# Splitting the virtual node's inner row over two PSUM banks, with three identity products behind it, in a four-network graph kernel

## The chip, the cores and the metric

The kernel is written in Bass and runs on one core of one Trainium2 chip. The metric is the device time of one launch in microseconds (us); lower is better.

## The reference, cut to what matters

Four graph networks run one after the other on 256 nodes of 512 features and 8192 edges, each between a layer norm and a residual add. Only the first one is touched by the change. It has seven layers; in each layer but the first, a "virtual node" gathers all nodes and gives one row of 512 numbers back to every node, ahead of the edge aggregation:

```python
for l in range(1, L):                       # L = 7
    h2 = relu(_ln(h, norm_g[l-1], norm_b[l-1]))
    vn_tmp = segment_sum(h2, batch) + vn                        # one row: sum over the nodes
    vn_hid = relu(_ln(vn_tmp @ vn_W1[l-1] + vn_b1[l-1], vn_g[l-1], vn_beta[l-1]))
    vn = vn_hid @ vn_W2[l-1] + vn_b2[l-1]
    h2 = h2 + vn[batch]
    h = _genconv(h2, src, dst, gcn_W[l], gcn_b[l]) + h          # softmax aggregation over edges, then a 512x512 product
```

All nodes are in segment 0 here, so `vn` is one row. Everything is float32.

## The kernel before, in words

Nodes lie in two tiles of 128 (`NT = 2`), features in four chunks of 128 (`CT = 4`). Adjacency is a dense 256x256 count matrix `cnt`, so that each sum over edges is a matrix product. Each engine has a program of its own, written out by hand in order, and they meet only through semaphores; SyncE (SP) issues the weight loads. There is no planner: what an engine does next is the next line of its program. In the listing all products of TensorE (PE) go through the helper `mm` and so carry line 762, all row picks of VectorE (DVE) line 1212.

One layer l (1 to 6) of the first network, `layer0` on each engine, goes like this:

1. PE begins the row `vn @ W1 + b1`: the bias (`vn_row_bias`) and chunk 0 of `vn` are already in the bank `row_bank(odd)` since the layer before; `vn_row_part(l, odd, 1, CT)` adds chunks 1 to 3. The column of `vn` is broadcast to a 128x128 stationary matrix, so every partition gets the whole row of 512.
2. `turn` transposes the normalised nodes `xn` (L797), tile by tile, as DVE has them ready (L1142). ScalarE (ACT) applies gain, bias and relu into `hT` and sums each chunk over the nodes into `hsum` (L645).
3. PE adds `hsum @ W1` to the row: four products of 512 columns, each with two records in the trace (tile `hsum`). Behind them it sets the bias of the next layer's row in the other bank (tile `ones`, one active row).
4. DVE, meanwhile, takes the maximum of `hT` over the nodes (L1226) and adds a bias (L1231). When the row is whole (`vn_hidden`) it takes its statistics (L1233, L1235), gives the variance to GpSimd (POOL) for the inverse root (L1236, L559), and picks from the row, which every partition has in full, each partition's own four numbers: `own_columns`, four multiply-and-sum instructions against the identity (L1212), each with a record that reads the accumulator. Three small operations follow (L1238, L1241, L1243), and `vhid` is ready (`vn_act`).
5. PE computes `vhid @ W2` in two halves of 256 columns, banks 2 and 3 (tile `vhid`, 16 records), each half raising `vn_half`.
6. For each half DVE picks `vn`, forms the shifts and the operand `md` (L1258); PE transposes `md` (`turn_md`, L871), and exponentials, the sums over edges, and the layer's 512x512 product (`conv`, banks 4 and 5) follow. DVE adds the result to `h` (L1148), tile 0 first, takes its statistics (L1115), and the next layer begins.

PE's wait between steps 4 and 5 is a wait for the chain of DVE. `keep_busy(bank, n)` exists already, for other places: n products of the identity with 256 columns into a bank that nobody reads.

Of the kernel before, what the change touches and what calls it, by code (L numbers as in the profile page):

```python
# [9 lines left out]
ALU = mybir.AluOpType  # L10
ACT = mybir.ActivationFunctionType
AX = mybir.AxisListType

P = 128
N = 256
NT = N // P
D = 512
CT = D // P
E = 8192
ET = E // P  # L20
LAYERS = 7
# [38 lines left out]
HALFWAY = 5  # L60
INDEG = 5
FILL_FIRST = 6

LN_EPS = 1e-5
MSG_EPS = 1e-7
# [32 lines left out]

TR_L2 = LAYERS
VN_OUT = 2  # L100


class Steps:
# [5 lines left out]
    def link(self, ins):  # L109

        self.mark(ins)
        self.await_marked()
# [19 lines left out]
def gnn_stack_kernel(nc, A, out):  # L132
    COL, NCOL_A, NCOL_B = column_table()
    ctx = ExitStack()
    with ctx:
        def sb(name, shape, dt=F32):
            return ctx.enter_context(nc.sbuf_tensor(name, shape, dt))
# [100 lines left out]
        vn = sb("vn", [P, CT])  # L238
        vhid = sb("vhid", [P, CT])
        vcen = sb("vcen", [P, CT])  # L240
        vst = sb("vst", [P, 6])
        vmv = sb("vmv", [P, 2])
        vvar = sb("vvar", [P, 2])
        scrap = region(5)[:, 0:CT * P].rearrange("p (c n) -> p c n", c=CT)
# [99 lines left out]
        def row_bank(odd):  # L344

            return 6 + odd
# [21 lines left out]
        def _(sp):  # L368
# [65 lines left out]
            with sp.Fori(1, LAYERS - 1) as l:  # L434
                conv_weights(l)

                sp.wait_ge(vn_hidden, l)
                sp.dma_start(wbuf[1], rows(A["L0_gnn_vn_W1"][bass.ds(l, 1)].rearrange("a k n -> (a k) n"))).then_inc(w_in[1], 16)
                sp.wait_ge(vn_half, l * 2)
                sp.dma_start(wbuf[2], rows(A["L0_gnn_vn_W2"][bass.ds(l, 1)].rearrange("a k n -> (a k) n"))).then_inc(w_in[2], 16)  # L440
# [2 lines left out]
            load_tab(0, 0)  # L443
            load_tab(1, 0)

            sp.wait_ge(vn_hidden, LAYERS - 1)
            load_w(1, A["L1_gnn_m_w1"][0], None)
            sp.wait_ge(vn_half, (LAYERS - 1) * 2)
            load_w(2, A["L1_gnn_m_w2"][0], A["L1_gnn_m_b2"][0])
# [310 lines left out]
        def _(pe):  # L760
            def mm(o, lhsT, rhs, start, stop):
                return pe.matmul(o, lhsT, rhs, start=start, stop=stop)  # L762
# [29 lines left out]
            def turn(tr, ready, value):  # L792

                for t in range(NT):
                    pe.wait_ge(ready, value + (t + 1))
                    for c in range(CT):
                        ins = pe.transpose(chunks(0)[:, c, t * P:(t + 1) * P], xn[:, t, c * P:(c + 1) * P], ident[:])  # L797
                        if t == NT - 1 and c % 2:
                            ins.then_inc(tr_done, 1)
# [20 lines left out]
            def column(col, c):  # L820

                return col[:, c:c + 1].to_broadcast([P, P])

            def vn_row_bias(l, odd):
                pe.wait_ge(b1_in, 16)
                mm(PS[:, row_bank(odd), :], ones[0:1, :], b1_rows[:, bass.ds(l * D - D, D)], True, False)

            def vn_row_part(l, odd, lo, hi):
                pe.wait_ge(w_in[1], l * 16)
                pe.wait_ge(vn_set, l * 2 - 1 if hi <= 2 else l * 2)  # L830
                for c in range(lo, hi):
                    mm(PS[:, row_bank(odd), :], column(vn, c), wbuf[1][:, c, :], False, False)

            def keep_busy(bank, n):

# [3 lines left out]
            def layer0(l, odd, first, last):  # L839
                if not first:  # L840
                    vn_row_part(l, odd, 1, CT)
                turn(l, ln_out, l * 2)
                if first:
                    keep_busy(4, FILL_FIRST)
                    pe.wait_ge(cnt_set, NT)
                    for s in range(NT):
                        ins = mm(PS[:, INDEG, 0:N], ones[:], cnt[:, s, :], s == 0, s == NT - 1)
                    ins.then_inc(indeg_done, 1)
                if not first:
                    for c in range(CT):  # L850
                        pe.wait_ge(hT_ready, l * CT + (c + 1))
                        ins = mm(PS[:, row_bank(odd), :], column(hsum, c), wbuf[1][:, c, :], False, c == CT - 1)
                    ins.then_inc(vn_hidden, 1)
                if not last:
                    vn_row_bias(l + 1, 1 - odd)
                if not first:
                    pe.wait_ge(w_in[2], l * 16)
                    pe.wait_ge(vn_act, l)
                    for b in range(2):
                        for c in range(CT):  # L860
                            ins = mm(PS[:, VN_OUT + b, 0:N], column(vhid, c), wbuf[2][:, c, b * N:(b + 1) * N],
                                     c == 0, c == CT - 1)
                        ins.then_inc(vn_half, 1)

                def turn_md(b):
                    pe.wait_ge(md_ready, l * 2 + (b + 1))
                    if b:
                        pe.wait_ge(mex_ready, l * 2 + 1)
                    for c in range(2):
                        for t in range(NT):  # L870
                            ins = pe.transpose(halves(row_bank(odd))[:, t, c * P:(c + 1) * P],  # L871
                                               md[:, 2 * b + c, t * P:(t + 1) * P], ident[:])
                    ins.then_inc(mdT_done, 1)

                def gather(bank, val, ready, done, b):
                    pe.wait_ge(ready, l * 2 + (b + 1))
                    for c in (2 * b, 2 * b + 1):
                        for t in range(NT):
                            ins = mm(chunks(bank)[:, c, :], val[:, t, c * P:(c + 1) * P], cnt[:, t, :], t == 0, t == NT - 1)
                    ins.then_inc(done, 1)  # L880

                turn_md(0)
                if not last:
                    vn_row_part(l + 1, 1 - odd, 0, 1)
                gather(0, ex, ex_ready, den_done, 0)
                turn_md(1)
                gather(2, mex, mex_ready, num_done, 0)
                gather(0, ex, ex_ready, den_done, 1)
                gather(2, mex, mex_ready, num_done, 1)

                if first:
                    pe.wait_ge(cond_s, 1)
                    mm(PS[0:NC, row_bank(0), 0:N], fw2[:], cz, True, True).then_inc(cond_b, 1)
                pe.wait_ge(w_in[0], l * 32 + 32)
                for b in range(2):
                    pe.wait_ge(z_ready, l * 2 + (b + 1))
                    for t in range(NT):
                        for c in (2 * b, 2 * b + 1):
                            ins = mm(PS[:, 4 + t, :], z[:, c, t * P:(t + 1) * P], wbuf[0][:, c, :], c == 0, c == CT - 1)
                        if b:  # L900
                            ins.then_inc(conv_done, 1)
# [202 lines left out]
        def _(dve):  # L1104
# [103 lines left out]
            def own_columns(bank, into, first, n):  # L1208

                for k in range(n):  # L1210
                    c = first + k
                    ins = dve.tensor_tensor_reduce(out=scrap[:, c, :], in0=PS[:, bank, k * P:(k + 1) * P], in1=ident[:],  # L1212
                                                   scale=1.0, scalar=0.0, op0=ALU.mult, op1=ALU.add, accum_out=into[:, c:c + 1])
                return ins
# [4 lines left out]
            def layer0(l, odd, first):  # L1219
# [3 lines left out]
                def par(name, at=0, n=CT):  # L1223
                    return cols[:, bass.ds(l * CT + (COL[name] - CT + at), n)]

                link(dve.tensor_reduce(hmax[:], hT[:], AX.X, ALU.max))  # L1226
                if first:
                    dve.tensor_copy(vn[:], cols[:, COL["vn_emb"]:COL["vn_emb"] + CT]).then_inc(vn_set, 2)
                    dve.wait_ge(vn_set, 2)
                else:  # L1230
                    link(dve.tensor_tensor(hmax_b[:], hmax[:], par("vn_b2"), ALU.add))  # L1231
                    dve.wait_ge(vn_hidden, l)
                    link(dve.bn_stats(vst[:], PS[:, row_bank(odd), :]))  # L1233
                    carry()
                    link(dve.bn_aggr(vmv[:], vst[:]))  # L1235
                    dve.tensor_scalar(vvar[:, 0:1], vmv[:, 1:2], LN_EPS, None, ALU.add).then_inc(vn_var, 1)  # L1236
                    link(own_columns(row_bank(odd), vcen, 0, CT))
                    link(dve.scalar_tensor_tensor(out=vcen[:], in0=vcen[:], scalar=vmv[:, 0:1], in1=par("vn_g"),  # L1238
                                                  op0=ALU.subtract, op1=ALU.mult))
                    dve.wait_ge(vn_est, l)  # L1240
                    link(dve.scalar_tensor_tensor(out=vhid[:], in0=vcen[:], scalar=vvar[:, 1:2], in1=par("vn_beta"),  # L1241
                                                  op0=ALU.mult, op1=ALU.add))
                    dve.tensor_scalar(vhid[:], vhid[:], 0.0, None, ALU.max).then_inc(vn_act, 1)  # L1243

                for b in range(2):
                    two = slice(2 * b, 2 * b + 2)
# [364 lines left out]
```

## Time and profile before

| | |
|---|---|
| median of 3 runs | 847.8 us (846.3 to 848.04) |
| the profiled execution | 845.63 us, its span 843.5 us |
| mean granted TensorE clock in it | 0.98 |
| PE busy | 779.4 us (92% of the span) |
| DVE busy | 601.8 us (71%) |
| first network, layers 1 to 6 | about 57 to 260 us of the span |

Times in rows are us from the start of the span unless marked ns. PE's records are modelled at their ends (a record lasts until its result has drained, so neighbours overlap), and a busy PE may run at half rate: the granted clock says so, 1.00 for 2.4 GHz and 0.50 for 1.2 GHz.

### The profile page before, as it was taken

To read this page: it belongs to the slowest core of one execution; us is meant where nothing else is said; L and a number is where in the kernel's file an instruction comes from. 1 tells how busy PE (TensorE), PEld (TensorE's weight loads), DVE (VectorE), ACT (ScalarE), POOL (GpSimd) and SP (SyncE) were. 2 spreads that over 40 slices of the span, in tenths; PEclk is the share of its full clock that TensorE was granted. 3 is DMA by queue.
4 is the path that set the end of the run, shared out by engine and by line. 5 is a ranking of instruction groups with operands and counts; after the bars stand their busy time and mean duration, and the time that the engine had idled before them with its cause. 6 is when DMAs were issued, how large, how long until landed. Compare 5 with 4: busy or idle time off the path is not lost.

```text
span 843.5 us, 10707 instructions
## 1 busy us (share of the span) xinstructions
PE 779.4 (92%) x3028; PEld 507.7 (60%) x3028; DVE 601.8 (71%) x1569; ACT 219.9 (26%) x458; POOL 127.5 (15%) x150
## 2 busy tenths in 40 slices
PE   6898898898888999999999999789999999999968
PEld 2556365364465765666667564466686585685753
DVE  8876575765767534544453563699999999999995
ACT  7632123122220311311311311502503404305200
POOL 5000000000011000000000001631351261341000
PEclk9899899999999999999999999999999999999989
DMA  5912314224131333423333100661632443330000
GB/s 165 347 63 100 113 52 159 86 76 162 62 126 70 122 109 119 162 99 137 119 112 113 63 1 16 194 214 51 187 113 79 133 138 101 103 97 0 1 1 25
DMA packets 39335, 88.39 MB, mean 105 GB/s; under 512 B 3986, under 2 KB 4319, under 8 KB 39295
## 3 DMA queue, kind: packets, MB, share of 16 engines
q1 hardware_dynamic: 34656, 72.72, 25.4%
q0 software_dynamic: 4640, 15.21, 6.1%
q8 instruction: 18, 0.29, 0.1%
q14 instruction: 21, 0.17, 0.1%
HBM read 86.86 MB, written 1.05 MB: 104 GB/s over the span
## 4 chain that ended last, share of the span: by engine, by line
PE 70%; DVE 14%; issue 11%; DVEq 3%; POOL 1%; ACT 1%; ACTq 0%; POOLq 0%
PE PS L762 41%; PE PS L1071 15%; PE PS L1057 11%; DVE big L1521 2%; DVE h L1148 1%; DVE tail L1512 1%; PE PS L922 1%; PE PS L771 1%; DVE x L1584 1%; DVEq L1484 1%; DVEq L1488 1%; PE PS L967 1%; PE PS L871 1%; PE PS L797 1%; DVE xn L1361 1%
## 5 line engine op out<-in xcount | busy, mean ns | idle before, releaser
L762 PE MATMUL PS<-big 128*128 128x512 f32 (+1 forms) x368 | 137.5, 524 | 1.9 <-DVE big L1412 1.7
L1512 DVE SCALAR_TENSOR_TENSOR tail<-big,coef 128x448 f32 (+3 forms) x208 | 125.1, 614 | 4.8 <-issue 4.5
L1521 DVE TENSOR_TENSOR big<-big,tail 128x448 f32 (+3 forms) x208 | 115.3, 554 | 3.6 <-DVE tail L1512 2.5
L762 PEld LDWEIGHTS PS<-big 128*128 128x128 f32 x368 | 67.4, 190 | 64.1 <-issue 54.8
L762 PE MATMUL PS<-hT,big 128*128 128x256 f32 (+1 forms) x512 | 87.0, 329 | 4.4 <-ACT hT L685 4.4
L583 POOL DMA_INDIRECT big<-h_rows,src_i x58 | 75.7, 1304 | 83.4 <-PE PS L1057 60.8
L762 PEld LDWEIGHTS PS<-hT,big 128*128 128x128 f32 x512 | 77.5, 191 | 15.2 <-ACT hT L685 7.3
L553 POOL TENSOR_TENSOR rstd<-var,minus_half 128x1 f32<-128x1 f32 x34 | 20.5, 605 | 417.3 <-DVE var L1122 417.2
L1057 PE MATMUL PS<-big,hotd_more 128*128 128x512 f32 x152 | 66.0, 592 | 0.0
L1071 PE MATMUL PS<-hotd_more,tail 128*128 128x256 f32 x280 | 63.1, 379 | 0.0
L1071 PE MATMUL PS<-hotd_more,prods 128*128 128x256 f32 x260 | 58.6, 379 | 0.0
L1071 PEld LDWEIGHTS PS<-hotd_more,tail 128*128 128x128 f32 x280 | 53.4, 191 | 7.4
L741 ACT ACTIVATE big<-consts 128x3584 f32<-128x3584 f32 x5 | 16.0, 3191 | 158.0 <-DVE big L1521 147.7
L1071 PEld LDWEIGHTS PS<-hotd_more,prods 128*128 128x128 f32 x260 | 49.4, 190 | 6.7
L762 PE MATMUL PS<-cnt,big 128*128 128x256 f32 x224 | 51.4, 382 | 0.8 <-ACT big L654 0.8
L1057 PEld LDWEIGHTS PS<-big,hotd_more 128*128 128x128 f32 x152 | 28.9, 190 | 36.4 <-issue 36.4
L1148 DVE TENSOR_TENSOR h<-PS,h 128x512 f32<-128x512 f32 x26 | 17.9, 689 | 44.3 <-PE PS L762 44.1
L762 PEld LDWEIGHTS PS<-cnt,big 128*128 128x128 f32 x224 | 41.4, 190 | 10.5 <-ACT big L654 5.5
L762 PE MATMUL PS<-big,hT 128*128 128x512 f32 x96 | 43.3, 597 | 2.6 <-ACT hT L685 2.0
L1377 DVE TENSOR_SCALAR big<-PS,cols 128x256 f32<-128x256 f32 x16 | 7.0, 479 | 52.7 <-PE PS L762 52.7
L1071 PE MATMUL PS<-xn,tail 128*128 128x256 f32 x128 | 32.8, 401 | 12.6 <-DVE tail L1531 11.5
L762 PE MATMUL PS<-big,vhid 128*128 128x256 f32 x96 | 29.9, 481 | 13.9 <-DVE vhid L1243 13.9
(208 smaller groups left out, 1063.7 us busy)
## 6 DMA issues: line engine op xcount, KB each, us to landing
big<-in_edge_attr_dram SPq DMA_DIRECT2D x32, 512.0 KB, 3.7
big<-in_L_gnn_vn_W_dram SPq DMA_DIRECT2D x12, 1024.0 KB, 5.3
big<-in_L_gnn_m_w_dram SPq DMA_DIRECT2D x8, 1024.0 KB, 5.4
big<-in_L_gnn_gcn_W_dram SPq DMA_DIRECT2D x7, 1024.0 KB, 5.3
big<-in_L_gnn_wv_dram SPq DMA_DIRECT2D x4, 1024.0 KB, 5.3
big<-in_L_gnn_wq_dram SPq DMA_DIRECT2D x4, 1024.0 KB, 5.4
big<-in_L_gnn_wk_dram SPq DMA_DIRECT2D x4, 1024.0 KB, 5.5
big<-in_L_gnn_wo_dram SPq DMA_DIRECT2D x4, 1024.0 KB, 5.3
```

The source lines that it names most:

```text
L553: pool.tensor_tensor(rstd[:, t:t + 1], var[:, t:t + 1], minus_half[:, t:t + 1], ALU.pow).then_inc(ln_est, 1)
L583: pool.indirect_dma_start(out=part[SOURCE_AT[g]][:, j, :], out_offset=None, in_=h_rows, in_offset=bass.IndirectOffsetOnAxis(ap=src_i[:, ti ...
L741: act.activation(cut, zero.to_broadcast([P, ZERO_CUT * D]), ACT.Copy).then_inc(acc_zero, 1)
L762: return pe.matmul(o, lhsT, rhs, start=start, stop=stop)
L771: ins = pe.matmul(PS[:, 2 + s, 0:N], hot_s[:, k, s * P:(s + 1) * P], hot_d[:, k, :], start=False, stop=True, skip_group_check=True)
L797: ins = pe.transpose(chunks(0)[:, c, t * P:(t + 1) * P], xn[:, t, c * P:(c + 1) * P], ident[:])
L871: ins = pe.transpose(halves(row_bank(odd))[:, t, c * P:(c + 1) * P], md[:, 2 * b + c, t * P:(t + 1) * P], ident[:])
L1057: ins = pe.matmul(PS[:, t, :], hotd(j)[:, t * P:(t + 1) * P], part[SUM_AT[g]][:, j, :], start=g == 0 and j == 0, stop=True, skip_group_che ...
L1071: ins = pe.matmul(set_bank(SETS - SETS_OF[g] + i), prods[n % 2][:, j, :], hotd(j), start=g == 0 and j == 0 and SETS - SETS_OF[g] + i != 3, ...
L1148: link(dve.tensor_tensor(to[:, t, :], PS[:, bank + t, :], to[:, t, :], ALU.add))
L1512: dve.scalar_tensor_tensor(out=prod[:, slot, tiles, :], in0=xs[:, tiles, bass.ds(i1, EXT)], scalar=coef[:, row:row + 1], in1=xe[:, tiles, ...
L1521: dve.tensor_tensor(o, o, prod[:, slot, tiles, :], ALU.add)._wait_ge(path_step, max(product_at[slot], added_at[0])).then_inc(path_step, 1)
```

## The change

The row of step 3 is computed as two halves of 256 columns. The first stays in `row_bank(odd)`, the second goes to bank 4 (`VN_SECOND`), whose last reader in the layer before is DVE's residual add of tile 0. Bias and the `vn` part of the second half (five products of 256 columns) are computed ahead of `turn`, after a wait for the statistics of tile 0 (`st_set`). The `hsum` products come in the order first half, second half, first, second, first, first, second, second, and each half raises `vn_hidden` once. DVE takes statistics and own columns of the first half while the second is under way, then the statistics of the second, the aggregate of both, and the own columns of the second. The maximum over `hT` and the bias add move behind `vhid`. PE gets three identity products ahead of its wait for `vhid` (bank 2, which the products of `vhid` overwrite). SP's waits count to double the number.

```diff
+FILL_ROW = 3
+VN_SECOND = 4
-        vst = sb("vst", [P, 6])
+        vst = sb("vst", [P, 2, 6])
-                sp.wait_ge(vn_hidden, l)
+                sp.wait_ge(vn_hidden, l * 2)
-            sp.wait_ge(vn_hidden, LAYERS - 1)
+            sp.wait_ge(vn_hidden, 2 * (LAYERS - 1))
...
             def vn_row_bias(l, odd):
-                mm(PS[:, row_bank(odd), :], ones[0:1, :], b1_rows[:, bass.ds(l * D - D, D)], True, False)
+                mm(PS[:, row_bank(odd), 0:N], ones[0:1, :], b1_rows[:, bass.ds(l * D - D, N)], True, False)
...
                 for c in range(lo, hi):
-                    mm(PS[:, row_bank(odd), :], column(vn, c), wbuf[1][:, c, :], False, False)
+                    mm(PS[:, row_bank(odd), 0:N], column(vn, c), wbuf[1][:, c, 0:N], False, False)
+
+            def vn_second_half(l):
+
+                pe.wait_ge(st_set, l * 2 + 1)
+                mm(PS[:, VN_SECOND, 0:N], ones[0:1, :], b1_rows[:, bass.ds(l * D - D + N, N)], True, False)
+                for c in range(CT):
+                    mm(PS[:, VN_SECOND, 0:N], column(vn, c), wbuf[1][:, c, N:2 * N], False, False)
...
                 if not first:
                     vn_row_part(l, odd, 1, CT)
+                    vn_second_half(l)
                 turn(l, ln_out, l * 2)
...
-                    for c in range(CT):
-                        pe.wait_ge(hT_ready, l * CT + (c + 1))
-                        ins = mm(PS[:, row_bank(odd), :], column(hsum, c), wbuf[1][:, c, :], False, c == CT - 1)
-                    ins.then_inc(vn_hidden, 1)
+                    for c, half in ((0, 0), (0, 1), (1, 0), (1, 1), (2, 0), (3, 0), (2, 1), (3, 1)):
+                        if half == 0:
+                            pe.wait_ge(hT_ready, l * CT + (c + 1))
+                        ins = mm(PS[:, VN_SECOND if half else row_bank(odd), 0:N], column(hsum, c),
+                                 wbuf[1][:, c, half * N:(half + 1) * N], False, c == CT - 1)
+                        if c == CT - 1:
+                            ins.then_inc(vn_hidden, 1)
                 if not last:
                     vn_row_bias(l + 1, 1 - odd)
                 if not first:
+                    keep_busy(VN_OUT, FILL_ROW)
                     pe.wait_ge(w_in[2], l * 16)
                     pe.wait_ge(vn_act, l)
...
-                link(dve.tensor_reduce(hmax[:], hT[:], AX.X, ALU.max))
                 if first:
+                    link(dve.tensor_reduce(hmax[:], hT[:], AX.X, ALU.max))
...
                 else:
-                    link(dve.tensor_tensor(hmax_b[:], hmax[:], par("vn_b2"), ALU.add))
-                    dve.wait_ge(vn_hidden, l)
-                    link(dve.bn_stats(vst[:], PS[:, row_bank(odd), :]))
+                    dve.wait_ge(vn_hidden, l * 2 - 1)
+                    dve.bn_stats(vst[:, 0, :], PS[:, row_bank(odd), 0:N])
+                    own_columns(row_bank(odd), vcen, 0, 2)
+                    dve.wait_ge(vn_hidden, l * 2)
+                    link(dve.bn_stats(vst[:, 1, :], PS[:, VN_SECOND, 0:N]))
                     carry()
-                    link(dve.bn_aggr(vmv[:], vst[:]))
+                    link(dve.bn_aggr(vmv[:], vst[:, :, :].rearrange("p a b -> p (a b)")))
                     dve.tensor_scalar(vvar[:, 0:1], vmv[:, 1:2], LN_EPS, None, ALU.add).then_inc(vn_var, 1)
-                    link(own_columns(row_bank(odd), vcen, 0, CT))
+                    link(own_columns(VN_SECOND, vcen, 2, 2))
...
                     dve.tensor_scalar(vhid[:], vhid[:], 0.0, None, ALU.max).then_inc(vn_act, 1)
+                    link(dve.tensor_reduce(hmax[:], hT[:], AX.X, ALU.max))
+                    link(dve.tensor_tensor(hmax_b[:], hmax[:], par("vn_b2"), ALU.add))
```

## Rows read from the trace of the kernel before

**Rows 1.** The page: the span, and the granted clock in 40 slices.
```profile
span 843.5 us, 10707 instructions
...
PEclk9899899999999999999999999999999999999989
```

**Rows 2.** Waits, layers 1 to 6: in total, times, longest.
```profile
PE PS L762 <- DVE vhid L1243: 13.9, 6, 3.1
```

**Rows 3.** Timeline of layer 3, from the hsum products to the transposes of md.
```profile
129.82 3.70 PE L762 MATMUL PS<-big,hsum 128*128 128x512 f32 x8 [0.74 <-ACT hT L645]
...
131.43 1.22 DVE L1226 TENSOR_REDUCE hmax<-hT 128x4 f32<-128x1024 f32 x1 [3.07 <-ACT hT L645]
...
133.45 1.12 PE L762 MATMUL PS<-big,ones 1*128 x2
133.62 0.70 DVE L1233 BATCH_NORM_STATS2 vst<-PS 128x6 f32<-128x512 f32 x1 [0.66 <-PE PS L762]
...
134.81 0.55 POOL L559 TENSOR_TENSOR vvar<-vvar,minus_half 128x1 f32<-128x1 f32 x1 [7.24 <-DVE vvar L1236]
...
136.66 3.69 PE L762 MATMUL PS<-big,vhid 128*128 128x256 f32 x16 [2.09 <-DVE vhid L1243]
138.66 0.29 DVE L1212 CUSTOM_DVE_ANT_0 big<-PS,ident 128x128 f32<-128x128 f32 x1 [2.15 <-PE PS L762]
...
140.66 0.65 PE L871 MATMUL PS<-ident,big 128*128 128x128 f32 x4 [0.31 <-DVE big L1258]
```

**Rows 4.** Timeline, layers 1, 2, 6: products of vhid, transposes of md, DVE's third pick.
```profile
69.12 5.38 PE L762 MATMUL PS<-big,vhid 128*128 128x256 f32 x16 [2.22 <-DVE vhid L1243]
74.34 0.60 PE L871 MATMUL PS<-ident,big 128*128 128x128 f32 x4
...
74.54 0.29 DVE L1212 CUSTOM_DVE_ANT_0 big<-PS,ident 128x128 f32<-128x128 f32 x1 [1.00 <-PE PS L762]
...
102.49 6.42 PE L762 MATMUL PS<-big,vhid 128*128 128x256 f32 x16 [2.30 <-DVE vhid L1243]
108.75 0.60 PE L871 MATMUL PS<-ident,big 128*128 128x128 f32 x4
...
233.65 5.38 PE L762 MATMUL PS<-big,vhid 128*128 128x256 f32 x16 [3.14 <-DVE vhid L1243]
238.87 0.60 PE L871 MATMUL PS<-ident,big 128*128 128x128 f32 x4
```

**Rows 5.** Stretches of layer 1: busy time by engine, granted clock, DMA share.
```profile
66.50:69.10 2.60, 0.40 (x1) 0.01 (x1) 2.07 (x15) 0.00 (x0) 0.55 (x1) 1.00 0.71 216
70.50:73.80 3.30, 3.30 (x9) 2.68 (x8) 1.81 (x10) 0.00 (x0) 0.00 (x0) 0.50 0.00 1
```

**Rows 6.** Groups of DVE by shape, layers 1 to 6: busy us, mean ns.
```profile
L1212 DVE CUSTOM_DVE_ANT_0 big<-PS,ident 128x128 f32<-128x128 f32 x48 | 11.6, 286 | 19.8 <-PE PS L762 19.8
...
L1258 DVE TENSOR_SCALAR big<-hT,shift,floor 128x256 f32<-128x256 f32 x24 | 8.8, 410 | 0.4
```

**Rows 7.** Timeline, the vn products and the transposes of xn, layers 1 and 2.
```profile
56.35 2.74 PE L762 MATMUL PS<-big,vn 128*128 128x512 f32 x6
...
57.28 1.29 DVE L1115 BATCH_NORM_STATS2 st<-h 128x6 f32<-128x512 f32 x2
...
60.12 1.27 PE L797 MATMUL PS<-ident,xn 128*128 128x128 f32 x8 [1.03 <-DVE xn L1142]
...
90.42 2.74 PE L762 MATMUL PS<-big,vn 128*128 128x512 f32 x6
93.05 0.66 PE L797 MATMUL PS<-ident,xn 128*128 128x128 f32 x4
94.03 0.66 PE L797 MATMUL PS<-ident,xn 128*128 128x128 f32 x4 [0.33 <-DVE xn L1142]
```

**Rows 8.** The page, DMA issues: line, count, KB each, us to landing.
```profile
big<-in_L_gnn_vn_W_dram SPq DMA_DIRECT2D x12, 1024.0 KB, 5.3
```

**Rows 9.** The tile vhid, weight loads: ns at the least, median, most.
```profile
L762 PEld LDWEIGHTS PS<-big,vhid x96: 185/190/338, 69.1 to 238.4; 128*128 128x128 f32 x96
```

## The prediction

> **What bounds the kernel now.** I read the page first. PE is busy for most of the span, and the granted clock reads 0.8 in three of the 40 slices, of 21.1 us each, and the fifth slice, 84 to 105 us, lies in the first network [rows 1]. That says that PE is the engine to follow, and that its clock isn't free. The waits of layers 1 to 6 come next: PE stands 13.9 us in six waits for `vhid`, 3.1 at the longest [rows 2]. The timeline of layer 3 shows the chain without disturbance: the `hsum` products run from 129.82, DVE does its maximum beside them after an idle 3.07 us, and takes the row's statistics at 133.62, 3.80 us later; `vhid` products start at 136.66, 6.84 us after `hsum`; the transposes of `md` start at 140.66, 4.00 us after that [rows 3]. Every step there waits for the one before, so the whole of it is on the path that sets the end.
>
> Last the clock. The same sixteen records of `vhid` take 3.69 us in layer 3 [rows 3] and 5.38, 6.42 and 5.38 in layers 1, 2 and 6 [rows 4]; layer 4 is like layer 1 (5.38) and layer 5 like layer 3 (3.69). The stretches say why: PE did 0.40 us of work in the 2.6 us ahead of the products of layer 1, and then ran at 0.50, 1.2 GHz, from 70.5 to 73.8 [rows 5]. So the idle hole costs twice, once by its own length and once, in four of six layers, by the clock behind it.
>
> **The change, part by part.**
>
> *1. Three identity products in the hole.* They are three products of 256 columns, two records each. Records of that shape start 0.216 us apart at full clock (3.69 us for sixteen, of which some 0.16 is the last one's drain and 0.08 the first one's start [rows 3]), so six take 1.3 us. They stand behind the bias product, which is now 256 columns wide and done some 4.2 us after the `hsum` start; the fill ends at about 5.6, and `vhid` comes (part 2) at 6.2. So they delay nothing. They leave PE idle for about 0.6 us instead of 2.1 to 2.3. Idle stretches of that length are in every layer, the 0.74 us ahead of `hsum` for one, and the `hsum` records behind it ran at full pace in layer 3 [rows 3]. I take it that the clock no longer falls in this place. What that gives is read from the transposes of `md`, the next thing that the path needs: they start 5.22, 6.26 and 5.22 us after the first `vhid` product in layers 1, 2 and 6 [rows 4], against 4.00 in layer 3 [rows 3]. The gain is 1.22 + 2.26 + 1.21 (layer 4) + 1.22 = 5.9 us. DVE's second half is let go earlier still (its third pick starts 5.42 us after the products in layer 1 [rows 4], and at full clock about 3.9), 7.3 us over the four layers, which bounds the gain from above; the sums over edges behind the first transposes keep PE busy, so most of that difference isn't on the path. From below the bound is nothing (first rival).
>
> *2. The row in two halves.* On PE the row costs the same: sixteen records at 0.216 for eight at 0.429, 3.55 us for 3.53. `hT` is no limit: ACT has the last chunk ready 1.6 us after the start, when DVE's maximum begins [rows 3], and it is first used at 2.3. The first half is done after twelve records, so DVE can start on it at 2.9 us, takes its statistics and two picks (0.21 us from start to start) and is free at about 3.75, just when the second half comes (3.82). What remains behind the row: statistics of 256 numbers for 512, two picks for four. The trace has no statistics of 256. An instruction of 128 columns takes 286 ns and one of 256 columns 410 [rows 6], the statistics of 512 take 0.70 [rows 3]; taking away 256 elements at the slope from 128 to 256 columns, 0.97 ns each, gives 0.45, near the row of 256 columns. Gain 0.25, with 0 (0.70) and 0.41 (0.29) as ends. Two picks fewer are 0.42. POOL's inverse root was done at 135.36 [rows 3], 0.98 us before the last of DVE's three small steps began and 0.7 before its use, so with 0.42 less beside it it stays covered. Aggregating twelve numbers for six is costed at nothing: with six it takes 0.18 us. Less 0.02 on PE, `vhid` comes 0.65 us earlier per layer (6.19 for 6.84), 3.9 us over six layers; ends 2.4 and 4.9.
>
> The Trainium skill, "VectorE: DVE Perf Modes", section on the TRN2 errata, has a price for such an instruction that no row here has: each pays a fixed extra, so that cutting one in two pays it twice, and a float32 add takes (N + 151)/0.96 ns, an estimated 0.42 us for each half. By it the gain would be 0.28 a layer, 0.2 us more in all, and the second fixed extra falls into the time of the first half, when DVE waits anyway.
>
> *3. The maximum over `hT` moved behind `vhid`* (1.22 and 0.16 us). It was covered before by PE's row; now the `vhid` products cover it. DVE waits 2.15 us there at full clock [rows 3]; the two take 1.45 with their links. Cost nothing, with 0.6 us to spare. Were the cover gone it would be 1.4 us a layer, but the `vhid` products can't come faster than in layer 3.
>
> *4. The second half's start, ahead of the transposes of `xn`.* Here PE gets more to do: three products of 512 columns become three of 256, plus bias and four of 256. In records: six at 0.429 = 2.57 us before; six at 0.216, two of bias, eight at 0.216 now. The bias with one active row is dearer at its edges: it starts 0.09 late behind `hsum` and its two records take 1.12 for a usual 0.43 + 0.59 [rows 3]. So 1.30 + 0.09 + 0.54 + 0.08 + 1.73 = 3.74 us. Before, the first tile's transposes followed the `vn` products at once (2.63 after their start) and the second tile's waited for DVE, at 3.61 [rows 7]. Now the first come at 3.79, the second 0.49 behind, at 4.28: 0.67 us later. That goes straight through ACT to `hsum`. Layers 2 to 6 agree in the 3.61 within 0.04, so 5 x 0.67 = 3.35 us lost. In layer 1 the transposes waited 1.03 us [rows 7]; the new wait for tile 0's statistics (57.28 + 0.69) holds the second half to 58.05, and the second tile's transposes come some 0.2 late. In the other layers those statistics end before the first `vn` product, and the wait is void. Behind PE's wait stand the transposes, and behind them ACT. Sum: a loss of 3.55 us; ends 2.5 (bias as cheap as the rest) and 5 (0.1 us more at each of two changes of shape, and the same in layer 1).
>
> *5. SP.* W1 of the next layer is still asked for at the end of the row (second increment, within 0.02 us). Asked for at 3.8 us after the `hsum` start and 5.3 us on its way [rows 8], it lands at about 9.2 with its issue, and is first used behind the transposes of `md`, now at 6.19 + 4.0 + 0.45 = 10.6. Cost nothing, with 1.4 us to spare.
>
> **Sum.** 5.9 + 3.9 - 3.55 = 6.25 us off the profiled execution: 845.63 to 839.4. That execution is 2.2 us below the median of the runs; the difference isn't explained by a row, so I carry the saving over to the median: 847.8 - 6.25 = 841.5.
>
> **The rivals.**
>
> *The clock falls all the same.* The hole is shorter but not closed, and the bias product next to it has one active row of 128. For it: the products of layer 2 lost more than those of the others, so its clock fell early, and other pauses (0.6 us in it, 0.7 ahead of `hsum`) remain. Against: layers 3 and 5 kept their clock with a 2.1 us hole, so the old hole is a marginal case and a third of it should be safe. Then only parts 2 and 4 count: 847.8 - 0.35 = 847.4, no change. 6 in 100.
>
> *The fill itself is late (slower than before).* If the clock has fallen by the time that the fill starts, its six records take 0.43 each, 2.6 us for 1.3, from 4.4 to 7.0, and `vhid`, ready at 6.19, stands behind them until 7.1, later than the 6.84 of now. PE's records stand in program order in every timeline, so nothing passes. It decides from the point where bias and fill together last more than 2.6 us behind the row. Then part 2 gives -0.26 a layer instead of 0.65, part 1 nothing: 847.8 + 1.6 + 3.55 = 853. Against: the clock was 1.00 in the hole of layer 1 [rows 5], and the row ahead of it is 3.5 us of solid work. 3 in 100.
>
> *Weight loads in the open.* The split doubles the loads of the row, 0.19 us each [rows 9]. If a load didn't lie beside the product ahead, the eight more behind `hsum` and the ten more ahead of `turn` would cost 18 x 0.19 = 3.4 us a layer, 20 us in all: 862. But sixteen loads of 0.19 and sixteen products of 256 columns took 3.69 us together in layer 3 [rows 3, 9], which leaves no room for it. 1 in 100. The Trainium skill, "TensorE: Matmul & The Clock Gate", section on packing small matmuls (what overlaps and what doesn't), says that a weight load overlaps running products only when the row group differs, which speaks against this change; these rows disagree with it, since the loads here use the whole array.
>
> *Both ends dear.* The statistics of a half cost as much as those of the whole, and part 4 costs 5 us: 5.9 + 2.4 - 5 = 3.3 saved, 844.5. Still faster. 4 in 100.
>
> **How the numbers follow.** My forecast, 841.5, has 86 in 100. A measurement of this kernel tells some 0.2% (1.7 us) from no change. Forecast and the last rival are faster, 0.90 in all; the first is the same, 0.06; the second and third slower, 0.04. The range takes the ends of the terms: 7.3 + 4.9 - 2.5 = 9.7 saved at most, of which I take most, to 838.5; at the other end 844.8, past both ends dear. The two runs' own scatter of 1.7 us lies in it. Beyond it are the first three rivals, 10 in 100, and some luck of the clock elsewhere.
>
> **What would show it.** PE's wait for `vhid` falls from 2.1 to some 0.6 us per layer; the `vhid` products take 3.7 us in all six layers, and their clock reads 1.00. `hsum` start to `vhid` product 6.2 us. Second tile's transposes 4.3 us after the first `vn` product for 3.6. Layers come some 32.0 us apart (layer 3 to 4 was 31.96, since parts 2 and 4 cancel), layer 1 to 2 and 2 to 3 too, where they were 33.3 and 34.4. The prediction is wrong if a granted clock of 0.50 still stands beside `vhid` products, if the fill ends behind `vhid`, or if DVE's picks of the first half end behind the second.

## The result, and the profile after

The changed kernel took 840.06 us (median of 4 runs, 839.34 to 841.16), beside 847.35 us for the kernel before on the same chip: a ratio of 0.9927, 95% interval 0.9906 to 0.9947. Two further series of the same kernel gave 0.9928 (0.9911 to 0.9945) and 0.9919 (0.9895 to 0.9942). The forecast was 841.5 us and a saving of 6.25 us. By the ratio the saving was 6.2 us (0.73% of 847.35), with 4.5 to 8.0 us as its interval; the two medians as they stand lie 7.3 us apart.

The page of the changed kernel, span and granted clock in 40 slices (tenths of full speed; PE is TensorE, DVE VectorE, ACT ScalarE, POOL GpSimd):

```profile
span 838.5 us, 11005 instructions
...
PEclk9999999999999999999999999899999999999989
```

Against [rows 1] the low digit of the first network's layers is gone. So is the one at 21 to 42 us, ahead of layer 1, which the change doesn't touch; in the profile of the third series it is back. A new one stands at 524 to 545 us, in the last network; it comes back below. The waits of layers 1 to 6, in total, times and longest, for [rows 2]:

```profile
DVE vst L1246 <- PE PS L764: 29.4, 6, 5.0
...
PE PS L764 <- DVE vhid L1259: 3.0, 6, 1.5
```

PE's wait for `vhid` went from 13.9 to 3.0 us: 0.30 us in five layers, 1.48 in the last, which has no bias product ahead of the fill and whose `vhid` comes 0.35 us later (last section). DVE's wait for the row is now 29.4 us, because the maximum, and the wait that stood ahead of it, no longer lie in between. The timeline of layer 3, from the `vn` products to the transposes of `md`, for [rows 3, 7]:

```profile
120.91 1.46 PE L764 MATMUL PS<-big,vn 128*128 128x256 f32 x6
...
122.29 0.69 PE L764 MATMUL PS<-big,ones 1*128 x2
...
122.92 1.99 PE L764 MATMUL PS<-big,vn 128*128 128x256 f32 x8
...
124.75 1.04 PE L799 MATMUL PS<-ident,xn 128*128 128x128 f32 x8
...
126.52 3.72 PE L764 MATMUL PS<-big,hsum 128*128 128x256 f32 x16 [0.74 <-ACT hT L647]
...
129.42 0.43 DVE L1246 BATCH_NORM_STATS2 vst<-PS 128x6 f32<-128x256 f32 x1 [4.97 <-PE PS L764]
...
130.28 0.43 DVE L1249 BATCH_NORM_STATS2 vst<-PS 128x6 f32<-128x256 f32 x1
...
130.80 1.56 PE L764 MATMUL PS<-iota_f,ident 128*128 128x256 f32 x6
...
132.42 1.21 DVE L1260 TENSOR_REDUCE hmax<-hT 128x4 f32<-128x1024 f32 x1
132.66 3.69 PE L764 MATMUL PS<-big,vhid 128*128 128x256 f32 x16 [0.30 <-DVE vhid L1259]
...
134.77 0.29 DVE L1226 CUSTOM_DVE_ANT_0 big<-PS,ident 128x128 f32<-128x128 f32 x1 [0.83 <-PE PS L764]
...
136.77 0.66 PE L885 MATMUL PS<-ident,big 128*128 128x128 f32 x4 [0.42 <-DVE big L1276]
```

Set each step against the kernel before: `hsum` to `vhid` products 6.14 us for 6.84; first `vn` product to `hsum` 5.61 for 5.01 (90.42 to 95.43 before); `vhid` products to the transposes of `md` 4.11 for 4.00. From one layer's `hsum` products to the next one's it is now 31.97 us, within 0.01 in all five cases; before it was 33.28, 34.39, 31.95, 33.09 and 31.96. Stretches of layers 2 and 4 of the changed kernel, to be read against [rows 5] (the stretch and its length; busy us of PE, of the weight loads, DVE, ACT and POOL; granted clock, DMA share, GB/s):

```profile
98.00:100.60 2.60, 2.39 (x10) 1.35 (x8) 2.17 (x16) 0.00 (x0) 0.55 (x1) 1.00 0.30 48
100.70:104.30 3.60, 3.60 (x16) 2.91 (x16) 2.48 (x11) 0.00 (x0) 0.00 (x0) 1.00 0.65 253
...
164.70:168.30 3.60, 3.60 (x16) 2.85 (x16) 2.48 (x12) 0.00 (x0) 0.00 (x0) 1.00 0.57 221
```

The products of `vhid` run at 1.00 in all six layers and take 3.69 us in each.

### The profile page after: what moved, and what is told of

It reads as the page before. It is cut to its first block, busy times and chain, and to the rows that moved or that the text cites. A ratio compares the mean times of both kernels' runs of the same rounds, so it can differ in the third digit from the quotient of the medians.

```text
span 838.5 us, 11005 instructions
## 1 busy us (share of the span) xinstructions
PE 784.4 (94%) x3172; PEld 530.8 (63%) x3172; DVE 601.4 (72%) x1575; ACT 220.0 (26%) x458; POOL 126.9 (15%) x150
## 4 chain that ended last, share of the span: by engine, by line
PE 74%; DVE 14%; issue 5%; DVEq 3%; ACT 2%; POOL 1%; ACTq 0%; another core or an unknown queue 0%; POOLq 0%
PE PS L764 44%; PE PS L1085 15%; PE PS L1071 11%; DVE big L1539 2%; PE PS L773 2%; DVE tail L1530 1%; PE PS L936 1%; DVE x L1602 1%; PE PS L885 1%; DVEq L1502 1%; PE PS L799 1%; DVEq L1506 1%; DVE big L1226 1%; PE PS L981 1%; DVE big L1276 1%
## 5 line engine op out<-in xcount | busy, mean ns | idle before, releaser
L687 ACT ACTIVATE hT<-PS 128x256 f32<-128x256 f32 x32 | 10.5, 381 | 115.2 <-PE PS L936 115.2
```

The lines of the kernel that those rows point to most:

```text
L687: act.activation(hT[:, some, t * P:(t + 1) * P], turned_tile(bank + t)[:, some, :], ACT.Copy).then_inc(yT_ready, 1)
```

## The experiments

### The fill and the split, each by itself

`fill_only` is the kernel before with the fill's one line (and its constant); `split_only` is the changed kernel without it:

```diff
                 if not first:
+                    keep_busy(VN_OUT, FILL_ROW)
                     pe.wait_ge(w_in[2], l * 16)
```

> The kernel before with nothing but the three identity products, ahead of its wait for vhid. Theory: the fill alone keeps the clock, and its gain and that of the split add up, so 5.9 us of the change's gain are here: 847.4 - 5.9 = 841.5 us, vhid products 3.7 us in all six layers, granted clock 1.00 beside them, hsum start to first vhid product still 6.84 us. Rival: the fill works only because the split makes the hole shorter; then the products still take 5.4 us in some layers and the time is 845 us or more.

> The changed kernel without the three identity products. Theory: the hole of PE is about 1.9 us (vhid at 6.14 us after hsum, bias done at 4.2) and the clock falls behind it in several of the six layers, so that only the split's own balance is left: 3.9 us won in DVE's chain, 3.3 us lost ahead of the transposes: 847 us, within 0.2% of the kernel before. Rival: the split itself gives most of the gain (a hole shorter by 0.3 us is enough for the clock): 842 us or less.

Measured: `fill_only` 843.61 us against 846.99, ratio 0.9955 (0.9942 to 0.9968); `split_only` 845.46 us, 0.9980 (0.9970 to 0.9990). In the profile of `fill_only` the `vhid` products take 3.69 us in all six layers, with `hsum` to `vhid` at 6.84 as before; the transposes of `md` in layer 6 start at 233.01 us, as against 238.87 [rows 4] and 233.03 in the changed kernel. Its last layer's rows:

```profile
229.01 3.69 PE L763 MATMUL PS<-big,vhid 128*128 128x256 f32 x16 [1.85 <-DVE vhid L1245]
233.01 0.66 PE L873 MATMUL PS<-ident,big 128*128 128x128 f32 x4 [0.32 <-DVE big L1260]
```

Layer 1 doesn't begin at the same time in every profile, so the difference is better counted from its first `vn` product (56.35 us before, 56.27 here, 56.55 in the changed kernel) to those transposes: 182.52 us before, 176.74 with the fill alone, 176.48 with the whole change. The fill alone has won 5.8 us, and the split 0.3 on top. In `split_only` the clock falls in layers 2, 4 and 6, behind holes of 1.79, 1.79 and 2.77 us. Its layer 2, products and stretches:

```profile
98.01 0.69 PE L764 MATMUL PS<-big,ones 1*128 x2
100.50 5.38 PE L764 MATMUL PS<-big,vhid 128*128 128x256 f32 x16 [1.79 <-DVE vhid L1258]
```
```profile
98.60:100.40 1.80, 0.11 (x1) 0.00 (x0) 1.43 (x11) 0.00 (x0) 0.55 (x1) 1.00 0.60 66
101.70:105.00 3.30, 3.30 (x10) 2.59 (x9) 1.74 (x11) 0.00 (x0) 0.00 (x0) 0.51 0.34 130
```

Three layers with a fall instead of four go with its being 0.2% faster than before; the mechanism expected is there. The one thing that does not fit is that the medians put the fill alone some 2 us behind the changed kernel, when its first network is only 0.3 us slower. So both went once more, on one chip:

> The fill alone once more, now on one chip with the changed kernel. Theory: the first network is as fast as in the changed kernel (first gather of the last network at 523.2 us in both), and the 2 us between their medians of before came from the last network (VectorE waited 1.9 us more for the sums of sets there, by luck of the clock), so here the two lie within 1 us of each other. Rival: the split is worth some 2 us over the fill alone, by a path that the one profile didn't show; then the fill alone is again 2 us or more behind the changed kernel.

> The changed kernel, beside the fill alone. Theory: 0.9928 of the kernel before as twice before, and within 1 us of the fill alone. Rival: 2 us or more ahead of it.

Measured: 841.46 us (0.9938, 0.9915 to 0.9961) and 839.25 us (0.9919, 0.9895 to 0.9942), 2.2 us apart, so the rival's number came, though not its path: no profile shows the split to be worth 2 us. Two of the six runs of the fill alone took 839.2 and 839.8 us, like the changed kernel, and four 841.3 to 842.0. This profile showed a place that the first one hadn't. Stretches of layer 1, first the waits round the transposes of `xn`, then the `hsum` products:

```profile
59.00:62.40 3.40, 1.68 (x9) 0.84 (x8) 1.50 (x6) 0.65 (x3) 1.17 (x2) 1.00 0.81 299
62.50:65.90 3.40, 3.40 (x4) 1.46 (x5) 1.38 (x2) 1.55 (x6) 0.00 (x0) 0.51 0.19 72
```

The `hsum` products took 5.37 us for 3.70 and `vhid` came 8.64 us after their start for 6.97. In the changed kernel PE does the second half's `vn` products in that pause. One more product there in the fill-only kernel should do the same:

```diff
                     vn_row_part(l, odd, 1, CT)
+                    keep_busy(VN_OUT, odd)
                 turn(l, ln_out, l * 2)
```

> The fill alone, and in odd layers one identity product more, behind the vn products and ahead of the transposes of xn (PE is idle there 1.0 us in layer 1 and 0.4 in layers 3 and 5). Theory: what the split adds to the fill alone is that its second half keeps PE busy ahead of layer 1's transposes, so that the clock doesn't fall behind them; with one product in that place the time is that of the changed kernel, 0.992 to 0.993 of the kernel before, hsum products 3.7 us in every layer, and its runs lie within 1.5 us of each other. Rival: the fill alone and this are alike, 0.994 to 0.9955, with some runs 2 us above the others.

Measured: 842.64 us against 847.52, 0.9940 (0.9922 to 0.9958), the six runs 842.05 to 843.41. Its layer 1 is clean (`hsum` to `vhid` 6.98 us, clock 1.00), its runs lie within 1.4 us as expected, but the time did not come down to the changed kernel's: the ratio is the rival's. So the fall in layer 1 cost that one execution its 2 us, and is not what holds the fill alone back in general.

The other two profiles part from the changed kernel's at the start of the last network. Waits of DVE between 515 and 600 us: `fill_only` first, then the changed kernel's third series, then `fill_both`:

```profile
DVE prods L1533 <- PE PS L1073: 1.9, 1, 1.9
```
```profile
DVE x L1487 <- PE PS L764: 1.3, 2, 1.1
```
```profile
DVE tail L1534 <- DMA big<-h_rows,src_i: 2.2, 1, 2.2
```

The line of the changed kernel is a wait that all three have; the other two it lacks. `split_only` has the first one too (2.0 us), so it isn't peculiar to the fill alone. In `fill_both` the first gather of node rows started late, because the write of those rows (`h_rows`), issued at 519.6 us in both, landed late; the rows of `fill_only` and `fill_both`:

```profile
523.21 1.21 POOL L584 DMA_INDIRECT big<-h_rows,src_i  x1 [3.57 <-DMA h_rows<-h]
```
```profile
525.45 1.21 POOL L584 DMA_INDIRECT big<-h_rows,src_i  x1 [5.81 <-DMA h_rows<-h]
```

And stretches of the same three there, in the same order:

```profile
534.00:538.00 4.00, 3.80 (x10) 3.07 (x11) 3.44 (x9) 0.00 (x0) 3.15 (x3) 0.58 0.89 285
```
```profile
534.00:538.00 4.00, 3.91 (x18) 3.47 (x19) 3.45 (x9) 0.00 (x0) 3.08 (x4) 1.00 0.90 276
```
```profile
534.00:538.00 4.00, 2.45 (x6) 2.01 (x7) 3.36 (x9) 0.00 (x0) 3.08 (x4) 0.65 0.87 305
```

Here too the clock falls in some executions, behind a pause of PE that no part of the change touches. The first profile of the changed kernel had the low clock there as well, from 533 to 540 us, and lost 1.0 us by it at the most: from the first gather to the end it took 315.3 us, the third series' profile 314.3, `fill_only` 316.7 and `fill_only_2` 314.3. So the three profiles of the fill alone lost their 2 us in three places: a fall of the clock in layer 1, a wait of DVE for PE in the last network, and a late write. The fill touches none of them; the split keeps PE busy in the first. Why the fill alone meets such a loss in most of its runs, and the changed kernel in none of its 15 (838.6 to 841.2 us), stays open: the split may help there in a way that no profile shows, or it was luck over three series each.

### The second half's place, and the maximum's

`spread` puts the second half's products where PE waits anyway; `max_first` moves the maximum and its bias add back ahead of the row's statistics.

```diff
+SPREAD = ((0, 1), (1, 2), (2, 4))
...
-                for c in range(CT):
+                vn_second_more(*SPREAD[0])
...
                     vn_second_half(l)
-                turn(l, ln_out, l * 2)
+                    for t in range(NT):
+                        pe.wait_ge(ln_out, l * 2 + (t + 1))
...
+                        vn_second_more(*SPREAD[t + 1])
```

> The changed kernel with the second half's five products spread: bias and the product of chunk 0 ahead of the first tile's transposes, chunk 1 between the two tiles, chunks 2 and 3 behind the second, where PE waits for VectorE and ScalarE. Theory: the 0.6 us a layer that the changed kernel loses ahead of hsum (first vn product to hsum 5.62 us for 5.01) come back, 3.2 us in all: 837 us, first vn product to hsum 5.0 to 5.1 us. Rival: the transposes are late for another reason, or the products behind them delay hsum as much: 840 us.

> The changed kernel with the maximum over hT back ahead of the row's statistics. Theory: it ends 3.05 us after the hsum start, against 2.9 for the first half's row, so VectorE is 0.15 us late for the second half and vhid comes 0.15 us later: 0.9 us in all, 841.0 us. Rival: the move costs or saves nothing measurable, 840.1 us; or it lay open before (1.4 us a layer), 848 us.

Measured: `spread` 839.54 us, 0.9908 (0.9895 to 0.9921). First `vn` product to `hsum` is 5.01 us in layer 2, as expected; but in layers 3 and 5 it is 5.41 and 5.37, since the first tile comes late there (DVE stands 0.4 us ahead of it in these two layers, the first in a turn of its loop), and the product put between the tiles delays the second. The last `hsum` products start at 220.56 us for 222.42: 1.9 us gained, or 2.3 counted from layer 1's `hsum`, of 3.2 expected. In the time of the runs that gain is not clear of the intervals. `max_first` 841.81 us, 0.9938 (0.9923 to 0.9952): `vhid` comes 6.40 us after `hsum` for 6.14, and DVE's pick of the first `vn` half 2.01 us after the `vhid` products for 2.11. Net 0.16 us a layer, 32.13 for 31.97 from layer to layer. The expected 0.15 was met by luck: `vhid` is 0.26 us late, and 0.10 comes back at the pick, which shows the 0.10 us that the moved maximum costs.

`spread_quiet` mends both places: odd layers take chunks 0 and 1 ahead of the first tile and nothing between the tiles, and GpSimd waits for the last `vhid` before it fills `tabw`.

```diff
+SPREAD = (((0, 1), (1, 2), (2, 4)), ((0, 2), (2, 2), (2, 4)))
...
             pool.wait_ge(vn_est, LAYERS - 1)
+            pool.wait_ge(vn_act, LAYERS - 1)
             pool.memset(tabw[0:2 * 32, :, :], 1.0).then_inc(tab_ones, 1)
```

> The changed kernel once more, unaltered, on the chip of the three others of this call. Theory: 0.9927 of the kernel before, as measured first, and 0.15% to 0.4% faster than the fill alone (0.9955), which it should lead by 0.3 us only if the two halves of the split balance as predicted. Rival: by the balance in the first network (first gather of the last network at 523.2 us in both profiles) it is no faster than the fill alone, and lies nearer 0.995.

> The second half's products spread round the transposes, with chunks 0 and 1 ahead of the first tile in odd layers (whose first tile comes late, at 3.1 us after the first vn product) and chunk 0 alone in even ones, and GpSimd's fill of tabw held back until the last vhid is ready. Theory: the layers come 31.36 us apart throughout (31.97 in the changed kernel), 3.0 us less, and the last vhid 0.35 us sooner: 840.1 - 3.3 = 836.8 us. Rival: odd layers stay at 31.7 us, 838 us; or the change round the transposes gives nothing here: 840 us.

> The spread second half with the late fill of tabw, beside the changed kernel on one chip. Theory: 3.3 us ahead of it, as its layers say; 0.988 to 0.989 of the kernel before. Rival: 4 us or more, as the medians of the call before had it.

Measured: `after_again` 839.58 us, 0.9928 (0.9911 to 0.9945); `spread_quiet` 835.70 us, 0.9883 (0.9860 to 0.9905), and the second time 836.00 us, 0.9885 (0.9857 to 0.9913), beside 839.25 for the changed kernel: 3.3 us, as forecast (3.9 the first time). The layers come 31.35 us apart in the mean, and in its layer 3 PE has no pause left from the `vn` products to the end of the row (from 120.8 us on):

```profile
120.80 1.24 PE L766 MATMUL PS<-big,vn 128*128 128x256 f32 x5
121.98 0.69 PE L766 MATMUL PS<-big,ones 1*128 x2
122.60 1.13 PE L766 MATMUL PS<-big,vn 128*128 128x256 f32 x4
123.73 1.11 PE L860 MATMUL PS<-ident,xn 128*128 128x128 f32 x8
124.68 1.03 PE L766 MATMUL PS<-big,vn 128*128 128x256 f32 x4
125.58 3.72 PE L766 MATMUL PS<-big,hsum 128*128 128x256 f32 x16
```

This is the version that beats both kernels, by 1.2% and 0.4%.

### What holds the clock

`fill_thin` makes the three fill products of one active row, `fill_one` keeps one of the three:

```diff
-                    keep_busy(VN_OUT, FILL_ROW)
+                    for _ in range(FILL_ROW):
+                        mm(PS[:, VN_OUT, 0:N], ones[0:1, :], iota_f[0:1, :], True, True)
```
```diff
-FILL_ROW = 3
+FILL_ROW = 1
```

> The changed kernel with the three fill products made of one active row (ones[0:1] by iota_f[0:1], 256 columns) instead of 128. Theory: what keeps the clock is that PE streams columns, whatever the rows: vhid products 3.7 us in all six layers, 840.5 us (0.2 us for the one-row loads are hidden in the hole). Rival: rows count; the clock falls as without a fill, vhid products 5.4 us in some layers, 845.5 us as without a fill.

> The changed kernel with one identity product for three, so that PE is idle some 1.4 us ahead of vhid. Theory: one is enough, since the kernel before kept its clock in two of six layers with a hole of 2.1 us: 840.1 us, vhid products 3.7 us in all layers. Rival: the clock falls in some layers, as without a fill (845.5 us): 842 to 844 us.

Both theories fell, and both rivals came, by ratio. `fill_thin`: 843.24 us, 0.9978 (0.9965 to 0.9991), which is `split_only`'s 0.9980 again. `fill_one`: 843.45 us, 0.9972 (0.9958 to 0.9986). Layer 2 of `fill_thin`, products, then stretches:

```profile
98.33 1.45 PE L764 MATMUL PS<-iota_f,ones 1*128 1x256 f32 x6
100.28 5.38 PE L764 MATMUL PS<-big,vhid 128*128 128x256 f32 x16 [0.50 <-DVE vhid L1260]
```
```profile
98.00:100.20 2.20, 1.79 (x8) 1.20 (x7) 1.79 (x12) 0.00 (x0) 0.55 (x1) 1.00 0.31 72
...
101.60:104.90 3.30, 3.30 (x10) 2.58 (x9) 1.73 (x10) 0.00 (x0) 0.00 (x0) 0.50 0.28 108
```

PE was idle for 0.50 us only and busy for 1.79 of 2.20 us. The clock still fell in layers 2, 4 and 6, the same ones as with no fill at all. Six records of the identity, with as many columns and 1.56 us for 1.45, held it behind this hole in all six layers of all ten profiles that have them, also where they left more idle time than this: 0.60 to 0.81 us in layers 1 to 5 of `fill_only`, and 1.85 in its layer 6. `fill_one` fell in layers 3, 4 and 6, behind 1.16, 1.16 and 2.34 us. Its layer 3:

```profile
132.71 5.38 PE L764 MATMUL PS<-big,vhid 128*128 128x256 f32 x16 [1.16 <-DVE vhid L1259]
```

One product differs from the other in its active rows and, with them, in what it multiplies; these runs don't part the two.

## Why the prediction was right

*The whole.* The mechanism of both big terms came as forecast. That the saving by the ratio lies within 0.1 us of the sum is luck, as its interval is 3.5 us wide. The profiles say it more sharply: from layer 1's first `vn` product to layer 6's transposes of `md` the change saves 6.04 us, for 6.25.

*The fill (5.9 us).* The step and its size hold: 5.8 us with the fill alone, against the four differences that were read from [rows 4] and the 4.00 of [rows 3]. The upper end from DVE's third pick (7.3) was rightly not taken. What was wrong is an argument for it: that the old hole was "a marginal case and a third of it should be safe". `split_only` fell at 1.79 us and `fill_one` at 1.16. The doubt that the prediction raised, the one-row bias product next to the hole, was the better thought: in `fill_thin` three products of one row didn't help. Whether the bias itself weighs anything wasn't tested. The fill also ends later than worked out, 5.84 us after the `hsum` start for 5.6, and leaves 0.30 us for 0.6.

*The split in DVE's chain (0.65 us a layer).* Measured 0.70 in layers 3 to 5: statistics of 256 numbers took 0.43 for the 0.45 worked out from [rows 6]. The formula for a float32 add in the Trainium skill, "VectorE: DVE Perf Modes", section on the TRN2 errata, an estimated 0.42, was the nearer, though these statistics are no add and read PSUM. In layers 1 and 2 it was 0.83 and 0.92 us, since `vhid` came later there before (6.97 and 7.06 us after `hsum` for 6.84); why isn't shown. In layer 6 only 0.35 us, for a reason that the prediction had not seen (GpSimd, below). Together 4.2 us for 3.9.

*The second half ahead of the transposes (3.55 us lost).* First `vn` product to the transposes 3.84 us for 3.79 worked out, and `hsum` 0.61 us later for 0.67: five times 0.61, and 0.2 in layer 1, make 3.3. `spread` shows that it is this and nothing else: with the products moved, the 5.01 us of before are back.

*The maximum at no cost.* Here the prediction is short by 0.1 us a layer. It said 0.6 us to spare, and DVE had 0.83, yet its pick starts 2.11 us after the `vhid` products for 2.00, and 2.01 in `max_first`. Why a covered instruction costs that isn't shown. The balance of the split is then 4.2 - 3.3 - 0.6 = 0.3 us, where it had been put at 0.35, and 0.26 is what the change gains over the fill alone. The sum came out by errors that cancel: 0.3 us more in layers 1 and 2 and 0.2 less lost by the second half, against 0.6 for the maximum.

*SP, and the loads beside the products.* W1 was never waited for. The row's sixteen records took 3.72 us for eight in 3.70, so the doubled loads are covered. The Trainium skill's sentence in "TensorE: Matmul & The Clock Gate", part on packing small matmuls, that loads overlap running products only where the row group differs, is not what these rows show, with 0.19 us of load beside each 0.216 us of product.

*The rivals.* "The clock falls all the same" did not come with three products, and did with one, and with three of one row; how near it was with three, no run tells. The late fill did not come: six records end 0.30 us ahead of `vhid`.

## What to carry to other kernels

A hole in PE's work is paid twice if the clock falls behind it, so read the duration of the same products in every repetition of a layer before pricing an edit, and take the difference between the fastest and the others as what the clock costs. Fill such a hole with products that use all rows, and check it by the granted clock: idle time alone did not tell here, where 1.85 us idle behind three full products kept the clock and 0.50 us behind three one-row products did not. And when work is added in front of a wait, split it and put the rest behind the wait: the same products cost 0.6 us a layer in one place and nothing in another.

## What had not been expected of the hardware

In this kernel one-row products kept PE busy in the records (1.79 of 2.20 us) and did not keep its clock: `fill_thin`, above.

Here a small operation of DVE was held by a memset of GpSimd. Layer 6 of the changed kernel:

```profile
227.79 0.94 POOL L564 MEMSET tail<- 64x1024 f32 x1
227.99 0.22 DVE L1257 SCALAR_TENSOR_TENSOR vhid<-vcen,vvar,cols 128x4 f32<-128x4 f32 x1
228.25 0.52 DVE L1259 TENSOR_SCALAR vhid<-vhid 128x4 f32<-128x4 f32 x1
```

The last step takes 0.52 us for 0.17 and ends, at 228.77, with the memset (228.73); the step before it, which has two tensor inputs, took its usual 0.22 beside the memset. The Trainium skill, "SBUF — State Buffer", section on SBUF's two separate sides, describes an exclusive lock on a port pair that the two engines share: whichever starts first holds it for its whole instruction, against DVE's operations in a two-port mode, while those with two SBUF inputs meet only GpSimd work that reads SBUF. Both rows agree with it, if the held step runs in a two-port mode, which no row shows. Before the change the memset ran from 232.47 to 233.41 and the same step began at 233.34, so only its end met it, and it took its usual 0.17 us. With the memset held back in `spread_quiet` the step took 0.17 us again and `vhid` came 6.13 us after `hsum` in layer 6 for 6.49.
